# Row norms of k and q: turned tiles squared by ScalarE with a row sum, in place of squares times a column of ones

## The reference

```python
def l2norm(x, eps=1e-6):
    return x * lax.rsqrt(jnp.sum(x * x, axis=-1, keepdims=True) + eps)

qkvz = hidden_states @ w_qkvz            # q, k, v, z
x = silu(causal_conv(concat(q, k, v), taps=4))
q = l2norm(q) * DK ** (-0.5)
k = l2norm(k)
for t in time:                            # the scan
    state = state * exp(g_t)
    delta = (v_t - state^T k_t) * beta_t
    state = state + k_t delta^T
    o_t = state^T q_t
y = rmsnorm(o * silu(z)) * norm_w @ w_out
```

## Time and profile before

| | |
|---|---|
| median of 3 runs | 3218.49 us (3217.93 to 3222.51) |
| profiled execution | 3209.48 us, its span 3207.7 us |
| busy share of the span | PE 91%, PEld 75%, DVE 92%, ACT 56%, POOL 69% |
| mean granted TensorE clock | 0.975 |
| PE, DVE busy from 1600 to 1900 us | 285.79 and 284.20 of 300 us |

### The profile page before, as it was taken

How to read it: one execution, slowest core, us unless ns; L and a number is a source line. 1 busy time by engine, 2 the same in 40 slices (tenths; PEclk the granted TensorE clock), 3 DMA queues, 4 the chain that set the end, 5 groups by cost and what they waited for, 6 DMA issues and landing times.

```text
span 3207.7 us, 56507 instructions
## 1 busy us (share of the span) xinstructions
PE 2926.0 (91%) x18444; PEld 2394.4 (75%) x18444; DVE 2951.7 (92%) x9293; ACT 1798.5 (56%) x4175; POOL 2218.9 (69%) x2394
## 2 busy tenths in 40 slices
PE   7942899999999999999999999999999999999997
PEld 4421678787878877878778877788787787877876
DVE  4997899999999999999999999999999999999996
ACT  3321555565556655565555655566555665656554
POOL 0003677877777777777777777787777777777764
PEclk9975999999999999999999999999999999999999
DMA  2002555555555555555555555555555565555653
GB/s 64 1 1 66 151 142 144 143 149 156 140 146 138 156 151 140 143 141 156 144 146 135 151 157 142 144 138 155 151 145 139 142 159 146 149 134 146 159 143 85
DMA packets 541829, 427.99 MB, mean 133 GB/s; under 512 B 247009, under 2 KB 450785, under 8 KB 541537
## 3 DMA queue, kind: packets, MB, share of 16 engines
q1 hardware_dynamic: 476000, 222.98, 25.6%
q0 software_dynamic: 65536, 201.39, 24.0%
HBM read 345.61 MB, written 45.09 MB: 122 GB/s over the span
## 4 chain that ended last, share of the span: by engine, by line
DVE 62%; PE 22%; ACT 8%; issue 5%; DMA 1%; POOL 1%; POOLq 1%; DVEq 0%; SPq 0%; ACTq 0%
DVE mix L1222 12%; DVE qkv L1181 9%; PE ps L584 4%; DVE E L1169 4%; DVE rows L1201 4%; PE ps L522 3%; DVE xg L1148 3%; PE ps L526 3%; PE ps L556 3%; PE ps L569 3%; PE ps L576 3%; DVE xr L1238 3%; ACT L824 2%; ACT L841 2%; DVE outer L1234 2%
## 5 line engine op out<-in xcount | busy, mean ns | idle before, releaser
L958 POOL DMA_INDIRECT rows<-table,idx_all x1024 | 1200.1, 1172 | 382.7 <-issue 280.3
L813 ACT ACTIVATE qkv<-qkv 128x512 f32<-128x512 f32 x256 | 161.4, 630 | 603.8 <-DVE qkv L1181 603.8
L942 POOL TENSOR_SCALAR xg<-xg,rms 128x128 f32<-128x128 f32 x520 | 407.3, 798 | 7.0
L576 PE MATMUL ps<-XT,E 128*128 128x128 f32 x3072 | 400.5, 277 | 0.0
L556 PEld LDWEIGHTS ps<-X,AT 128*128 128x128 f32 x3072 | 363.4, 192 | 35.7 <-DMA X<-whole 17.9
L1222 DVE SCALAR_TENSOR_TENSOR mix<-rows,zc,mix 128x256 f32<-128x256 f32 x896 | 381.3, 491 | 0.4 <-ACT zc L824 0.4
L556 PE MATMUL ps<-X,AT 128*128 128x128 f32 x3072 | 375.2, 275 | 3.3 <-DMA X<-whole 3.3
L576 PEld LDWEIGHTS ps<-XT,E 128*128 128x128 f32 x3072 | 368.7, 192 | 0.0
L946 POOL COPY gn<-gates 128x8 f32<-128x8 f32 x64 | 12.3, 193 | 481.3 <-SPq L330 262.2
L950 POOL TENSOR_SCALAR gm<-cst,gn 128x128 f32<-128x128 f32 x512 | 340.3, 680 | 6.5
L808 ACT ACTIVATE raw<-ps 128x512 f32<-128x512 f32 x256 | 152.9, 597 | 313.5 <-PE ps L522 313.5
(11 more groups left out here) (165 smaller groups left out, 6172.5 us busy)
## 6 DMA issues: line engine op xcount, KB each, us to landing
Wvz<-wvz SPq DMA_DIRECT2D x64, 512.0 KB, 3.2
xb<-xnT SPq DMA_DIRECT2D x64, 512.0 KB, 4.5
whole<-AT SPq DMA_DIRECT2D x128, 256.0 KB
X<-whole SPq DMA_DIRECT2D x128, 256.0 KB, 4.2
XT<-whole SPq DMA_DIRECT2D x128, 256.0 KB, 4.7
wo<-woh SPq DMA_DIRECT2D x65, 256.0 KB, 4.4
Wkq<-wkq SPq DMA_DIRECT2D x64, 256.0 KB, 2.9
rows<-table,idx_all POOLq DMA_INDIRECT x1024
```

The source lines that it names most:

```text
L576: done = mm(ps[:, 4 + g, (a % 4) * P:(a % 4 + 1) * P], E[:, a, :], src[:, a, :], start=True, stop=True)
L942: pool.tensor_scalar(xg[:, a, :], xg[:, a, :], rms[:, a:a + 1], None, ALU.mult).then_inc(sm["y_p"], 1)
L958: pool.indirect_dma_start(rows[:, m, :], None, table[:, :], bass.IndirectOffsetOnAxis(ap=idx_all[:, f // 4, c:c + 1], axis=0)).then_inc(ga ...
```

## The change

The matmul with ones goes. TensorE instead transposes the four 128x128 blocks of k (then of q) into PSUM (`turns`), so that a token is a partition; ScalarE squares each block from PSUM and lets the activation's second output sum the row (`row_squares`), four instructions per call; VectorE reads the four sums from SBUF instead of PSUM. The 128x512 squares in `silu` are gone. Three waits change: VectorE's two ss instructions wait for ScalarE (`sq_s`) and no longer for TensorE (`ss_t`), and TensorE reuses banks 7 and 6 when ScalarE has read them (`sq_s`), no longer when VectorE has read the four columns (`ssk_v`).

```diff
-                def squares(w, bank):
-                    pe.wait_ge(sm["sq_s"], at("sq_s", w + 1))
+                def turns(w, bank):
                     for t in range(4):
-                        done = mm(ps[:, bank, t:t + 1], sq[:, w, t * P:(t + 1) * P], ones[:, 0:1], start=True, stop=True)
+                        done = pe.transpose(ps[:, bank, t * P:(t + 1) * P], qkv[:, w, t * P:(t + 1) * P], ident)
                     done.then_inc(sm["ss_t"], 1)
...
-                    squares(0, 7)
+                    turns(0, 7)
                     pe.wait_ge(sm["km_v"], at("km_v", 1))
                     projection(1)
...
-                    pe.wait_ge(sm["ssk_v"], at("ssk_v", 1))
+                    pe.wait_ge(sm["sq_s"], at("sq_s", 4))
                     products(1, 7)
                     pe.wait_ge(sm["tap_s"], at("tap_s", 4))
-                    squares(1, 6)
+                    turns(1, 6)
...
-                    pe.wait_ge(sm["ssk_v"], at("ssk_v", 2))
+                    pe.wait_ge(sm["sq_s"], at("sq_s", 8))
                     projection(3)
...
                     A(qkv[:, u, :], qkv[:, u, :], ACT.Silu).then_inc(sm["silu_s"], 1)
-                    if u < 2:
-                        act.wait_ge(sm["silu_s"], at("silu_s", u + 1))
-                        A(sq[:, u, :], qkv[:, u, :], ACT.Square).then_inc(sm["sq_s"], 1)
+
+                def row_squares(w, bank):
+                    act.wait_ge(sm["ss_t"], at("ss_t", w + 1))
+                    for t in range(4):
+                        A(sq[:, w, t * P:(t + 1) * P], ps[:, bank, t * P:(t + 1) * P], ACT.Square,
+                          accum_out=ssr[:, w, t:t + 1]).then_inc(sm["sq_s"], 1)
...
                     take_XT(0, 1)
+                if front:
+                    row_squares(0, 7)
+                if back:
                     act.wait_ge(sm["xg_v"], at("xg_v", 2))
                     squares(1)
...
+                if front:
+                    row_squares(1, 6)
+                if back:
                     silu_scores(1)
...
-                    dve.wait_ge(sm["ss_t"], at("ss_t", 1))
-                    V.tensor_scalar(ss[:, 1, :], ps[:, 7, 0:4], 1e-6, None, ALU.add).then_inc(sm["ssk_v"], 1)
+                    dve.wait_ge(sm["sq_s"], at("sq_s", 4))
+                    V.tensor_scalar(ss[:, 1, :], ssr[:, 0, :], 1e-6, None, ALU.add).then_inc(sm["ssk_v"], 1)
...
-                    dve.wait_ge(sm["ss_t"], at("ss_t", 2))
-                    V.tensor_scalar(ss[:, 0, :], ps[:, 6, 0:4], float(P), P * 1e-6, ALU.mult, ALU.add).then_inc(sm["ssk_v"], 1)
+                    dve.wait_ge(sm["sq_s"], at("sq_s", 8))
+                    V.tensor_scalar(ss[:, 0, :], ssr[:, 1, :], float(P), P * 1e-6, ALU.mult, ALU.add).then_inc(sm["ssk_v"], 1)
```

More of the change, by code:

```diff
@@ L169, in program @@
         per = dict(proj_t=6, diff_t=2, kk_t=2, ss_t=2, e_t=6, x_t=4, xt_t=6, v_t=3, y0_t=1, yt_t=2, s_t=1, o0_t=1, ks_t=2,
-                   y1_t=1, o1_t=1, out_t=2, silu_e=2, exp_done=2, tap_s=8, x_s=4, xt_s=6, silu_s=4, sq_s=2, sumsq_s=8,
+                   y1_t=1, o1_t=1, out_t=2, silu_e=2, exp_done=2, tap_s=8, x_s=4, xt_s=6, silu_s=4, sq_s=8, sumsq_s=8,
                    rv_s=8, S_s=1, qs_s=4, z_s=2, yT_s=2, dot_v=2, xg_v=4, e_v=6, conv_v=4, km_v=1, kq_v=1, ssk_v=2,
@@ L243, in program @@
         ss = sb("ss", [P, 2, 4])
+        ssr = sb("ssr", [P, 2, 4])
         rk2 = sb("rk2", [P, 4])
```

## The result

The changed kernel takes 3301.01 us, the median of 4 runs (3299.02 to 3304.76), against 3218.21 us of the kernel before: ratio 1.026, 95% interval 1.0241 to 1.0278. A second set (experiment 11) gave 3297.34 against 3211.15 us, ratio 1.027 (1.0252 to 1.0288). The profiled execution took 3302.19 us with a span of 3300.4 us and a mean granted clock of 0.960, where it was 0.975. The two profiled executions differ by 92.7 us. From the first km to the last it is 82.1 us (2905.9 in place of 2823.7) and behind the last 2.1; the other 8.5 us lie ahead of the first km, at 309.18 us in place of 300.65. They are not the change's: in the profile of the second set the first km is at 300.20 us.

What follows compares the result with a forecast made beforehand. DVE (VectorE) was taken to bound the kernel between km and RV; 56 x 1.35 + 7 x 0.9 + 1.8 for the front = 84 us, added to 3218.5, gave 3302 us, with an 8-in-10 range of 3266 to 3345.

Steps and rivals of the forecast that it cites:

- What bounds the kernel: Between km and RV only DVE (VectorE) sets the pace; a delay there moves the next pass by the same amount.
- The saving: At both norms, PE saves about 0.5 us a call, 1.0 us a pass, worth 0 on the path.
- First wait, 0.96 us: At the norm of k, DVE finishes km and stands 0.96 us until ScalarE's last row sum lets ss start.
- the stated bounds: ScalarE's row squares from PSUM: spacing from 0.29 us less a few hundredths up to 0.30 + 0.19, 2.0 us for four.
- Second wait, 0.39 us: At the norm of q, ss waits another 0.39 us for row squares queued on ScalarE behind RV and Kd.
- Minus a few hundredths: Deduction from the two waits' 1.35 us a pass, for the small gap at level(2).
- 1.35 us a pass: Sum of DVE's two waits at the norms of k and q, 0.96 + 0.39, charged in 56 passes.
- The rival: After the norm of k, less PE work makes the clock fall more often: 3323 to 3365 us, chance 0.12.
- The profile-after list: Signs expected in the later profile, such as km to km 45.9 us; half-clock windows well over seven would contradict the forecast.
- The rule on transposes: At the norms, transposes take about 275 ns and don't engage full clock, supporting the clock rival's 3323 to 3365 us.

Runs made afterwards that it cites:

- experiment 11: The changed kernel measured once more, unaltered: 3297.34 us against 3211.15 us of the kernel before, ratio 1.027.
- experiment 1: The kernel before with two extra VectorE instructions (about 0.43 us each) between km and ss: 3245.4 us, ratio 1.0098.
- experiment 4: The changed kernel with only the norm of q by transposed tiles, that of k by squares and ones as before: 3302.47 us, ratio 1.0267.
- experiment 3: The changed kernel with only the norm of k by transposed tiles, that of q by squares and ones as before: 3228.32 us, ratio 1.0055.
- Experiment 2: The changed kernel with two extra 128x512 matmuls on PE ahead of its wait for Y before the Kd product: 3255.88 us, ratio 1.0132.
- experiment 5: The changed kernel with one extra 128x512 matmul on PE ahead of its wait for Y before the Kd product: ratio 1.0353 to the kernel before.
- experiment 6: The changed kernel with VectorE's convolution taps of k moved ahead of the last two steps of expert_mix(0): ratio 1.0624 to the kernel before.
- experiment 7: The changed kernel with earlier k taps, q's row squares between the halves of Kd, and two extra matmuls before PE's wait for Y: ratio 1.0499.
- experiment 8: The changed kernel with only the norm of k by transposed tiles, and the taps of k moved earlier: ratio 1.0436 to the kernel before.
- experiment 9: Three of VectorE's eight expert dots moved between km and ss: ratio 1.0112 with only k's norm by transposed tiles, 1.0501 in the changed kernel.
- experiment 10: The kernel before with one extra 128x512 matmul on PE ahead of the k products: 3222.82 against 3237.49 us, ratio 0.996.

## Why the prediction was right, and where it was luck

The forecast was 3302 us and the measured time 3301. The mechanism was right, and the closeness of the number was in part two errors that cancel.

- **What bounds the kernel.** Right. A delay of VectorE between km and RV moves the pass (experiment 1), and PE's saving is worth nothing: PE's busy time fell and its pause grew. The saving itself was put too high, 0.5 us a call where the trace has 0.95 - 0.60 = 0.35; at a value of 0 that did no harm.
- **First wait, 0.96 us.** There, 0.82: the row squares stand 0.25 us apart with PSUM as source, inside the stated bounds.
- **Second wait, 0.39 us.** In a regular pass 0.31, and ss moved by 0.39 us against the end of kq. The reason given was right for the full change; alone, that side costs twice as much (0.78), since RV then waits for PE (experiment 4). That PE sets none of the times in this chain held only because VectorE was late.
- **"Minus a few hundredths."** This term failed. Of 1.21 us of later starts only 0.88 are in the pass: neg takes 0.14 us after a later ss and 0.28 before, the four triangle instructions behind it 1.14 in place of 1.19, and `level(2)` with the dots had 0.14 us of slack to PE, which the earlier trace rows don't show and the chain of waits hid. Experiments 1 and 3 show the same: 0.34 of 0.86 and 0.35 of 0.82 us come back. So 1.35 us a pass was 0.88, some 30 us too much over 63 passes. Why neg is shorter after a later ss, no run shows.
- **The clock.** The rival was given 0.12 and counted for the norm of k, where the turns were to starve PE. Falls in half of the passes came, but in another place and for another reason: none right after km, 30 behind the pause ahead of Kd. They cost 1.29 us in each of those passes, 39 us in all, where the seven of the kernel before cost 1.6 us each, 11 in all. That is about 28 us more, and it closes the gap that the last point opened: 55 us of delay and 28 of clock are 83, where the forecast had 84 of delay and none of clock. This agreement is luck. Experiment 2 shows that the pause is needed for them: with it filled, 45.44 us in nearly all passes. The prediction had no term for it, though the pause ahead of Kd stands in the earlier trace rows. The profile-after list did name half-clock windows above seven as a sign against the forecast, and by that sign it was not confirmed.
- **The rule on transposes.** The Trainium skill (TensorE: Matmul & The Clock Gate, Part 4: PE-mode transpose) says that the full clock doesn't engage for them. The traces don't bear this out at the norm of k. At nearly the same regular pass, 45.07 and 45.02 us, the kernel of experiment 1, with ones-matmuls there, has 15 half-clock stretches right after km and that of experiment 3, with transposes, none. All kernels with ones-matmuls there and no filler have some (7, 15 and 17), no kernel with transposes there has one at that place. At Kd the traces can't say, since filling the pause was enough. The 275 ns for a transpose, which the prediction quotes too, fit: a record of `turns` lasts 0.27 us.
- **What stays open.** Why the clock falls in every second pass when PE's pause ahead of Kd is 2.17 us in each. Over experiments 1 to 5 and the changed kernel, none of the pauses there of up to 1.57 us had a half-clock stretch behind it and about half or more of those from 2.07 us up had; lengths between are missing, and at the norm of k 0.95 us was enough at times. Nor is it shown what makes ScalarE's copies start late in experiments 5 to 9.

## What to carry to other kernels

Moving a reduction from TensorE to ScalarE takes work off one engine and puts a longer chain in front of the engine that waits for the result; look at which instruction is next in that engine's queue, not at busy shares. When the bounding engine gets later, price the pauses of TensorE that this makes. What they cost in clock was half of the delay itself here (28 and 55 us), and filling them with matmuls that nobody needs took the half-clock stretches away in experiments 2, 5 and 10. And when two halves of a change wait on one chain, test each alone: here one half cost 0.55% and the other 2.7%, and together they cost 2.6%. A mean over passes of two kinds can hide both: 1.87 us was the mean of pauses of 1.56 and of 2.07 to 2.38.

## What the hardware showed that was not expected

- Squares with a row sum start every 0.25 us from PSUM and every 0.29 us from SBUF, 128x128 f32 each.
- Extra matmuls made a kernel faster twice: by 45 us in the changed kernel (two medians of different sets; as ratios to the kernel before 1.026 and 1.0132) and by 0.4% in the kernel before.
- The clock fell in two quite different places: 0.5 to 1.3 us behind a pause of 2.17 us ahead of Kd, and 2 to 3 us behind one of 0.95 us at the norm of k, there with ones-matmuls and never with transposes.
- Four one-column f32 matmuls, eight records in 0.95 us, cost more of PE than four full 128x128 transposes, four records in 0.60 us.
